# A second attention layer pair re-laid with tokens on partitions: queries and keys projected, rotated and normalised per tile of 128 tokens, then turned

## The reference

```
def rmsnorm(x, w): return x * rsqrt(mean(x*x) + 1e-6) * w
def qk_norm(x):    return x * rsqrt(mean(x*x over the head's 16 numbers) + 1e-6)

def global_latent_attn(x, wq, w_kv_down, w_k_up, w_v_up, wo):
    q = split_heads(x @ wq, 16);  latent = x @ w_kv_down          # 64 wide
    k = split_heads(latent @ w_k_up, 4);  v = split_heads(latent @ w_v_up, 4)
    q, k = rope(q, 1e6), rope(k, 1e6);  q, k = qk_norm(q), qk_norm(k)
    return merge_heads(sdpa(q, repeat4(k), repeat4(v), causal)) @ wo

def local_gqa_attn(x, wq, wk, wv, wo):   # the same with k = x @ wk, v = x @ wv, base 1e4

x = hidden
x = x + global_latent_attn(rmsnorm(x, norm1_w), ...)
x = x + local_gqa_attn(rmsnorm(x, norm2_w), ...)
```

## Time and profile before

| | before |
|---|---|
| median of 3 runs | 344.79 us |
| profiled execution, its own time | 344.11 us |
| its span (first to last instruction) | 342.3 us |
| PE busy | 323.1 us (94%), 3508 products |
| DVE busy | 221.3 us (65%) |
| ACT busy | 173.2 us (51%) |
| POOL busy | 148.3 us (43%) |
| mean granted PE clock, share of full | 0.99 |

### The profile page before, as it was taken

The page is one execution under the profiler, slowest core; times in us unless marked ns, Lnnn a source line. Parts: engine busy times, 40 slices in busy tenths (PEclk is TensorE's granted clock), DMA queues, the critical chain, the costliest instruction groups (busy, mean ns, idle before and its releaser), DMA issues.

```text
span 342.3 us, 8467 instructions
## 1 busy us (share of the span) xinstructions
PE 323.1 (94%) x3508; PEld 270.2 (79%) x3508; DVE 221.3 (65%) x577; ACT 173.2 (51%) x370; POOL 148.3 (43%) x167
## 2 busy tenths in 40 slices
PE   7999899998879989999999999997989899898996
PEld 5785578876479989999999999997557686676864
DVE  1099798997887444556555554556955788666774
ACT  0304674557233255766676666533038870586700
POOL 5201019900607847888798889864600001000020
PEclk9999999999989999999999999998999999999999
DMA  7991003320022173575766764165000000000002
GB/s 261 404 394 62 3 0 98 88 87 3 0 95 83 58 232 105 188 232 189 228 202 199 223 182 161 45 204 213 1 0 2 2 4 3 0 1 4 4 2 71
DMA packets 16016, 37.09 MB, mean 108 GB/s; under 512 B 1930, under 2 KB 9729, under 8 KB 15976
## 3 DMA queue, kind: packets, MB, share of 16 engines
q1 hardware_dynamic: 14576, 33.68, 29.6%
q0 software_dynamic: 960, 2.43, 2.3%
q10 hardware_dynamic: 440, 0.41, 0.5%
HBM read 30.76 MB, written 5.75 MB: 107 GB/s over the span
## 4 chain that ended last, share of the span: by engine, by line
PE 63%; DVE 18%; ACT 6%; POOL 5%; issue 4%; DMA 3%; POOLq 0%; ACTq 0%; SPq 0%; DVEq 0%
PE ps L1551 10%; PE ps L1552 9%; PE ps L1553 9%; PE ps L1749 5%; PE ps L1338 3%; POOL xg_d L1296 3%; PE ps L1759 3%; PE ps L1845 2%; PE ps L1821 2%; PE ps L1350 2%; DMA xgs<-xg_d 2%; ACT stage_l L475 1%; DVE stage_l L840 1%; PE ps L1882 1%; DVE mx L834 1%
## 5 line engine op out<-in xcount | busy, mean ns | idle before, releaser
L1253 POOL TENSOR_TENSOR w0l<-raw,w0h 128x384 fp32r<-128x384 f32 (+1 forms) x60 | 56.3, 972 | 13.0 <-ACT w0h L541 12.7
L1269 POOL TENSOR_TENSOR rstd<-vtmp,cst 128x3 f32<-128x3 f32 (+1 forms) x8 | 6.7, 838 | 111.0 <-DVE vtmp L739 58.7
L1030 DVE TENSOR_TENSOR ps<-gact,ps 128x256 f32<-128x256 f32 (+3 forms) x60 | 26.3, 438 | 35.7 <-ACT gact L565 34.8
L1253 POOL TENSOR_TENSOR w1l<-raw,w1h 128x384 fp32r<-128x384 f32 (+1 forms) x48 | 44.8, 974 | 6.7 <-ACT w1h L541 5.8
L565 ACT ACTIVATE gact<-ps 128x256 f32<-128x256 f32 (+3 forms) x60 | 23.2, 387 | 19.9 <-PE ps L1553 19.4
L569 ACT ACTIVATE hrh<-ps 128x256 fp32r<-128x256 f32 (+1 forms) x48 | 18.4, 383 | 28.0 <-DVE ps L1030 28.0
L1035 DVE TENSOR_TENSOR hrl<-ps,hrh 128x256 fp32r<-128x256 f32 (+1 forms) x48 | 20.4, 424 | 18.4 <-ACT hrh L569 18.4
L1338 PE MATMUL ps<-cst 128*128 128x512 f32 x62 | 27.9, 595 | 0.0
L1551 PE MATMUL ps<-xg0h,w1h 128*128 128x256 f32 x88 | 25.8, 293 | 0.0
L1551 PE MATMUL ps<-xg1h,w0h 128*128 128x256 f32 x88 | 25.7, 292 | 0.0
L1552 PE MATMUL ps<-xg1l,w0h 128*128 128x256 f32 x88 | 24.9, 283 | 0.0
(11 more groups left out here) (301 smaller groups left out, 926.1 us busy)
## 6 DMA issues: line engine op xcount, KB each, us to landing
raw<-in_wexp SPq DMA_DIRECT2D x18, 768.0 KB, 4.4
raw<-in_wexp SPq DMA_DIRECT2D x9, 640.0 KB, 4.7
xg_d<-zero SPq DMA_DIRECT2D x8, 256.0 KB, 10.7
xgs<-xg_d SPq DMA_DIRECT2D x8, 256.0 KB, 5.0
stage_l<-in_xT SPq DMA_DIRECT2D x6, 320.0 KB, 5.1
yg_d<-y SPq DMA_DIRECT2D x7, 256.0 KB, 4.1
stage_l<-in_tokW SPq DMA_DIRECT2D x6, 128.0 KB, 5.2
wq_l<-in_wql SPq DMA_DIRECT2D x1, 640.0 KB, 5.3
```

What stands on the lines that cost most here:

```text
L1030: V.tensor_tensor(up, gact[i % 2][rows_of(c), 0:n], up, ALU.mult).then_inc(S("hm"), 1)
L1253: last = nc.gpsimd.tensor_tensor(wset[i][1][w], raw[w], wset[i][0][w].bitcast(F32), ALU.subtract)
```

## The change

Queries and keys come out with tokens on partitions. For each of the five tiles PE takes 128 columns of `xnT` as the stationary operand and the joined weight of queries and keys, 320 columns wide, as the moving one. A head has 16 columns now. DVE makes both products of the rotation in one pass of 640 columns (`rotate`), adds them in two passes of 160 (`add_halves`), sums the squares that ACT made (`sum_squares`), and multiplies by the inverse roots into a zeroed tile with 32 columns for each head (`normalise`); PE turns that tile by five transposes (`turn_qk`), and ACT copies it out of PSUM as `qT` and `kT` (`take_turned`). The products for the mean squares and folded keys are gone, and so are the latent and the buffer `km`: at the start of li = 0 PE multiplies the two key/value weights together (`kvd_s`, `kvu_s`), ACT copies the result behind the query weight, and li = 0 then runs as li = 1. The values are projected in two halves of eight images, between turns; ACT, not DVE, copies them. The residual passes stand behind the last `normalise` but one, and are one per tile in both layers. Two products of filler became the weight product: `keep_clock` 9 became 8. POOL's one large memset of `km` went, and two of 640 columns (`blank`) stand ahead of the last step of `wfs`. SP's nine DMAs are other ones in another order.

```diff
@@ PE, l1(li)
-                keep_clock((9, 4)[li], (0, 7)[li])
+                if li == 0:
+                    pe.wait_ge(S("d_l1"), 16 * 9)
+                    for k in range(DC):
+                        last = M(bank(1)[:, k * 2 * KV * DH:(k + 1) * 2 * KV * DH], kvd_s[:, k * P:(k + 1) * P],
+                                 kvu_s[:, :], start=True, stop=True, skip_group_check=True)
+                    last.then_inc(S("wkv_mm"), 1)
+                keep_clock((8, 4)[li], (0, 7)[li])
                 transposes(li + 2)
                 pe.wait_ge(S("nT"), 2 * (li + 2))
...
+                def project(t):
+                    if t >= 2:
+                        pe.wait_ge(S("rot2"), n0 + t - 1)
+                    for k in range(DC):
+                        last = M(bank(QKB[t % 2])[:, 0:QK], xnT[:, k, t * P:(t + 1) * P], w["wq"][:, k, :],
+                                 start=(k == 0), stop=(k == DC - 1))
                     last.then_inc(S("qk_mm"), 1)
...
+                def turn_qk(t):
+                    pe.wait_ge(S("qkn"), n0 + t + 1)
+                    if t >= 1:
+                        pe.wait_ge(S("qT"), 2 * (n0 + t))
+                    for u in range(KV):
+                        nc.tensor.transpose(bank(6)[:, u * P:(u + 1) * P],
+                                            normed[t % 2][:, u * P:(u + 1) * P], ident)
+                    nc.tensor.transpose(bank(7)[:, 0:P], normed[t % 2][:, KV * P:(KV + 1) * P], ident).then_inc(S("t_mm"), 1)
 
                 def scores(grp):
-                    if grp == 0:
-                        pe.wait_ge(S("qkn"), U * li + U // 2)
...
+                    pe.wait_ge(S("qT"), 2 * (n0 + grp + 2))
...
-                for grp in range(5):
+                project(0)
+                project(1)
+                project(2)
+                project(3)
+                project_values(range(0, B // 2))
+                turn_qk(0)
+                project(4)
+                turn_qk(1)
+                project_values(range(B // 2, B))
+                turn_qk(2)
+                scores(0)
+                turn_qk(3)
+                turn_qk(4)
+                for grp in range(1, 5):
                     if grp < 4:
                         scores(grp)
-                    if grp >= 1:
-                        values(grp - 1)
+                    values(grp - 1)
@@ ACT, l1(li)
+                square(0)
+                square(1)
+                inverse_root(0)
+                square(2)
+                inverse_root(1)
+                take_turned(0)
+                square(3)
+                inverse_root(2)
+                take_turned(1)
+                square(4)
+                inverse_root(3)
+                take_values()
+                take_turned(2)
+                inverse_root(4)
+                take_turned(3)
+                exponentials(0)
+                take_turned(4)
...
+                for grp in range(1, 4):
+                    exponentials(grp)
+                    inverse(grp - 1)
                 inverse(3)
@@ DVE, l1(li)
+                def rotate(t):
+                    dve.wait_ge(S("qk_mm"), n0 + t + 1)
+                    if n0 + t:
+                        dve.wait_ge(S("rot"), 2 * (n0 + t))
+                    V.tensor_tensor(turn2[0].rearrange("p (a j d) -> p a j d", a=2, d=DH),
+                                    by_head(bank(QKB[t % 2])[:, 0:QK]).unsqueeze(1).to_broadcast([P, 2, QK // DH, DH]),
+                                    rot_s[:, li, t, :]...to_broadcast([P, 2, QK // DH, DH]), ALU.mult).then_inc(S("rot2"), 1)
...
+                rotate(0)
+                add_halves(0)
+                rotate(1)
+                add_halves(1)
+                sum_squares(0)
+                for t in range(2, TT):
+                    rotate(t)
+                    normalise(t - 2)
+                    add_halves(t)
+                    sum_squares(t - 1)
+                sum_squares(TT - 1)
+                normalise(TT - 2)
+                residual(0)
+                normalise(TT - 1)
+                for t in range(1, TT):
+                    residual(t)
@@ POOL
-            nc.gpsimd.memset(km[:, :, :, :, :], 0.0).then_inc(S("zeros"), 1)
...
+                    pool.wait_ge(S("expert_done"), E + 1)
+                    for x in normed:
+                        nc.gpsimd.memset(x, 0.0).then_inc(S("blank"), 1)
```

More of the change, by code:

```diff
@@ L70 @@
 C_CSK = C_CSQ + N
[L71 to L73 removed]
+C_MASK = C_CSK + T
 C_HM = C_MASK + N
@@ L317, in tiles @@
             return range(BATCH[i].start, BATCH[i].stop)
[L321 to L334, removed]
+        QKB = (4, 5)
         LAST = (4, 5, 6, 3, 7)
@@ L638, in take_keys @@
[L638 to L650, removed]
@@ new lines, in take_turned, with take_values @@
+                def take_turned(t):
+                    act.wait_ge(S("t_mm"), n0 + t + 1)
+                    A(qT[:, :, t * P:(t + 1) * P], bank(6).rearrange("p (u c) -> p u c", u=KV), ACT.Copy).then_inc(
+                        S("qT"), 1)
+                    A(kT[:, t * P:(t + 1) * P], bank(7)[:, 0:P], ACT.Copy).then_inc(S("qT"), 1)
+                def take_values():
+                    act.wait_ge(S("v1_mm"), li + 1)
+                    for e in range(2):
+                        r = slice(KS * e, KS * e + N)
+                        last = A(vo[r, :, :, e, :].rearrange("p b g d -> p (b g) d"),
+                                 bank(3)[r, :].rearrange("p (c d) -> p c d", d=DH), ACT.Copy)
+                    last.then_inc(S("vo"), 1)
@@ new lines, in exponentials @@
+                def exponentials(grp):
+                    for g in range(KV):
+                        act.wait_ge(S("s_mm"), 16 * li + 4 * grp + g + 1)
+                        if grp >= 2:
+                            act.wait_ge(S("o_mm"), 4 * li + grp - 1)
+                        A(ex[grp % 2][:, g, :], bank(g)[:, 0:QT], ACT.Exp,
+                          scale=0.25).then_inc(S("ex"), 1)
+                square(0)
+                square(1)
+                inverse_root(0)
+                square(2)
@@ L1142, in l1, with residual @@
                 if li == 0:
[L1143 removed]
                     V.memset(ozp[:, :, T:TP], 0.0).then_inc(S("pads"), 1)
[L1145 removed]
+                def residual(t):
+                    if li == 0:
                         V.tensor_scalar(xres[:, t, :], h[:, t, :], mv[:, t, 0:1], roots[:, 0, t:t + 1],
                                         ALU.subtract, ALU.mult).then_inc(S("res"), 1)
[L1148 to L1150 removed]
@@ L1176, in l1 @@
-                for u in range(U + 3):
-                    if u < U:
-                        rotate(u)
-                    if u >= 3:
-                        normalise(u - 3)
-                    if u == 7:
-                        dve.wait_ge(S("zeros"), 2)
-                        take_keys(0)
-                    if u == U:
-                        take_values()
-                take_keys(1)
+                    else:
+                        V.tensor_tensor(h[:, t, :], h[:, t, :], xres[:, t, :], ALU.add).then_inc(S("h_half"), 1)
```

251 lines of the change are left out of this document (102 added, 149 removed).

## The result

The changed kernel takes **332.38 us** (median of four runs, 329.99 to 334.57), the kernel before 345.18 beside it (340.32 to 345.95): ratio 0.970, 95% interval 0.963 to 0.976. The ratios in this document are of fast executions alone, those within 1.5% of the fastest of their kernel, so they are not quotients of the medians. The change gives back some 10 us, and faster was the forecast: 330.5, in a range of 326.5 to 336.5, for a gain of 14.3. The execution profiled took 329.99 us, 1.8 above its span.

What follows compares the result with a forecast made beforehand. PE was taken to bound both second-tower layers' start-ups, with DVE and ACT setting the time afterwards. 344.1 - 14.0 (7.0 per layer) - 0.3 = 329.8, given as a median of 330.5 us, range 326.5 to 336.5.

Steps and rivals of the forecast that it cites:

- start-up: Start of each second-tower layer, from xnT complete to group 2's first exponential; forecast to shorten by 7.0 us per layer.
- A round of DVE: DVE's passes for one tile (rotate, two adds, sum of squares, normalise), 2.45 us less overlaps: put at 2.05 us.
- root(4): ACT's inverse roots for the last tile in each layer; named as what is late, ending at 13.42 us.
- normalise(4): DVE's multiplication of the last tile by its inverse roots; put at 13.45 to 13.94 us, behind root(4).
- turn(4): PE's transposes of the last tile; said to follow normalise(4) and to wait for turn(3)'s copy until 14.71 us.
- PE's waits: PE's idle times inside each layer's start-up, ahead of scores(0), turn(3) and turn(4): 0.4, 0.3 and 1.0 us.
- Marker: First exponential of attention group 2 in each layer; forecast 19.2 us behind T0 against 26.2 before.
- The 2% added for the count's shortness: Counting the kernel before gave 25.7 us against 26.2 traced, so the new start-up's 18.8 was raised to 19.2.
- T0: End of the copy that completes `xnT` in each second-tower layer; the forecast's times count from it.
- An unchanged pace of 2.33 us a group: Assumed for the attention groups behind the start-up: PE's 1.17 + 1.16 us per group stays as before.
- Rival 2: PE's clock falls once per layer near 13 us behind T0, costing 1.5 us each, 333.5 us; chance 0.17.
- the third case: Short access runs are slow on DVE: five rounds each 0.64 us longer, 3.2 per layer, 337 us; chance 0.10.

Runs made afterwards that it cites:

- half_values: Changed kernel with the values contracted over half the features (one product of two, results wrong), 64 PE records fewer per layer; start-up 0.4 us shorter.
- dve_extra: Changed kernel with one more DVE pass per tile, a copy of 320 columns behind `add_halves` that nobody reads; start-up 0.57 us longer.
- km_memset: Changed kernel with POOL's removed memset of `km` put back at the start, on a buffer nobody reads; 337.89 us, ratio 0.969 to the kernel before.
- best: Changed kernel with tile 3's turn in its own banks ahead of `scores(0)`, and values copied by DVE; 336.8 us against 350.18 before, ratio 0.961.
- filler_turns: Changed kernel with each filler product of the second tower and last block replaced by seven fp32 transposes of 128 columns; start-ups 19.4 us.
- the like pair: The quick-starting execution of the unchanged kernel before (span 338.9 us) beside the changed kernel's first profile (span 328.2); difference 10.7 us.
- pad: Changed kernel with PE's filler ahead of both layers cut into products of 64 columns, moving later instructions down the stream; 365.74 us, start-ups 19.4.

## Why the prediction was right, and where it was not

- **The bound.** The start-up fell from 26.2 to 19.4 us because PE no longer holds it end to end. "PE no longer sets the time: DVE and ACT do" is right but for 0.4 us: two us less of PE's work give that much (*half_values*), 1.15 us more of DVE's cost 0.57 (*dve_extra*), and PE still holds 5.1 us of the chain in the middle. A round of DVE was put at 2.05 and took 2.00; the last took 2.32, with the wait for the last projection, which the count did not have.
- **What is late next was named wrongly.** The prediction says in bold type that it is root(4), with normalise(4) and turn(4) behind it. The chain goes another way: root(3), the two copies of the values, turned(2), turn(3), turned(3), turn(4). Normalise(4) ends 0.85 us before turn(4) starts. The prediction's own list of PE's waits had this right (turn(4) waits for the copy of turn(3), 14.71), so the sum did not suffer by the sentence. PE's waits were forecast at 0.4, 0.3 and 1.0 us, ahead of scores(0), turn(3) and turn(4). The timeline has none, 0.15 and 0.95 there, and 0.18 ahead of the third projection.
- **The prices.** DVE within 0.01 us each. The overlap of neighbours was read as 0.08 from four passes of 416 ns in 1.32 us; these give 0.11. ACT's root was put at 2 x 0.22, after the row of an exponential of 40 columns, and its first pass, L628, takes 0.31. The value copies were put at 0.65, and take 0.59. Marker: 19.2 forecast, 19.4 measured; the gain per layer 6.8 instead of 7.0. The 2% added for the count's shortness was luck in part. What the count lacks here is a later first `rotate` (T0 + 1.44, put at 1.27), the wait for the last projection (0.23) and the dearer root (0.09), and a count of the kernel before could tell nothing of these.
- **Covered edits.** POOL's memsets take 1.19 us for two, and nobody waits; *km_memset* shows the other end. The residual passes run up to the first mask, and PE's values do not wait. T0 came 0.2 earlier (0.3 forecast).
- **The failed assumption: "An unchanged pace of 2.33 us a group".** From the marker to the next T0 the kernel before takes 15.3 and 14.8 us, the changed one 15.9 and 15.6, and over all of its variants up to 16.9. The table shows why: where a layer has no stop, it takes 15.3 and 14.8 again (*half_values*, first layer; *dve_extra* and *best*, second; but *half_values* 15.0 in its second), and a layer with stops takes their length and 0 to 0.5 us more, mostly 0.3. That extra is not explained. The prediction had named this as the place that it did not look at. Loss: 0.9 us per layer at most in this execution, 1.4 in both.
- **The clock did fall, elsewhere.** Rival 2 had it fall at T0 + 13, 1.5 us each time. The start-ups behind T0 had 1.00 throughout. But in the last block, behind the last T0 (317.07):

```profile
318.00:321.00 3.00, 3.00 (x8) 2.39 (x8) 0.80 (x2) 0.00 (x0) 0.00 (x0) 0.52 0.00 0
```

 The final products take 5.41 us there, and 3.72 in the kernel before. Timelines of the two, the changed kernel first:

```profile
318.06 5.41 PE L1894 MATMUL ps<-wfs,xnT 128*128 128x256 f32 x16
```
```profile
330.46 3.72 PE L1882 MATMUL ps<-wfs,xnT 128*128 128x256 f32 x16
```

 In 9 of the 12 profiles of changed kernels in the table the last block takes 9.0 instead of 7.3 us, and in neither of the two of the kernel before. The fall begins 0.85 to 2.2 us behind the last T0 in all nine. PE was busy at 2.4 GHz for 10 us ahead of it: the output's projection, filler, ten transposes and then, directly ahead, four products over a single partition (eight records, 1.9 us). The kernels without a fall, and the kernel before, have the same (only *filler_turns* has transposes for filler). What brings it about was not tested, and with two profiles of before I can't tell whether the change favours it; this stays open.
- **The sum, for the like pair:** 0.2 (T0) + 6.3 + 5.9 (from T0 to T0) - 1.7 (last block) = 10.7 us, the difference of the spans. Forecast were 14.3. The forecast time is 1.9 us below the measured median and well inside the range; of the 3.6 us of gain that are missing in the pair, the longer groups (1.4) and the clock (1.7) make 3.1. That the first pair showed 14.1 was luck: it came from the clock at the start, not from a sum that was right. The range's upper end was said to be the third case, 336.5; that case was put at 337.

## What to carry to other kernels

When the bound of a start-up moves from one engine to others, count the new chain engine by engine with durations from like-sized rows: 19.2 against 19.4 us came out. Read the engine that is late from the list of waits, not from the story told of it: here the two differed, and the list was right. Then ask what the faster part leads into: here PE ran into its own instruction fetch, which no row of before showed as a wait. And compare marks inside the program before believing a difference between two spans: 3.5 us of the first pair was the clock at the start.

## What the runs showed of the hardware that I had not expected

- PE's instructions come in 16 KB blocks of 127 loads and 127 products. Of the 26 stops 20 end 3.4 to 4.0 us behind the edge of the block before, the others, with waits in between, 4.5 to 6.1; dense groups (64 records in 1.17 us) use a block up in 2.8 to 3.6. Whether there is a stop also varies from execution to execution (0.28 or 0.84 us at one place), and the kernel before, with groups just as dense, showed none in two profiles. There the edges at loads 2723 and 3358 come 2.9 to 3.1 us behind the start of a packet, so it was in time; what makes a fetch late is open. In *pad*, five blocks end between the first layer's second stop and the one in the second layer, and none of them shows a stop.
- 228 records of 64 columns took 25.5 us, 0.11 each: cutting 512 columns at 0.43 into narrow pieces costs twice as much or more per column.
- PE's first ten records of a 39-partition product took 2.4 us in three executions and 4.6 in eleven. It is the clock: 256 columns took 0.43 us until 12.3 to 15.5 us in the eleven, the pace at the lower level. The row of the granted clock shows 1.00 for a stretch of which the trace has no entry, so durations have to be looked at there.
- The fall of the clock near the end came in 9 of 14 profiles, behind 10 us of a busy PE and not behind a wait.
